# A two-block kernel on one core: weights loaded in exchanged 32-wide blocks and turned in place by VectorE, and the attention's constants made in the second group

## What is computed

```python
xn = _layernorm(x)
s = _L0_attn_ref(xn, W_in, W_out, A_theta, B_real, B_imag, C_real, C_imag, norm_w)
g = _silu(_L0_ffn_ref(xn, W1, W2, W3))   # silu(xn W1^T) * (xn W3^T), Walsh-Hadamard transform over 1024, times W2^T
x = x + s * g
xn = _layernorm(x)
s = _L1_attn_ref(xn, qkv, o_proj, gamma, beta)   # causal softmax attention
g = _silu(_L1_ffn_ref(xn, W1, W2, W3))
x = x + s * g
```

## Time and profile before

| | |
|---|---|
| time, median of 3 runs | 363.39 us (362.97 to 363.65) |
| time of the profiled execution | 363.3 us |
| its span | 361.5 us |
| TensorE busy | 355.8 us, 98% |
| VectorE busy | 250.6 us, 69% |
| ScalarE busy | 169.2 us, 47% |
| GpSimd busy | 100.8 us, 28% |
| granted TensorE clock | 1.0 in every slice (2.4 GHz, the upper level) |
| DMA packets | 42336, of which 5700 under 512 B; 38.63 MB |

### The profile page before, as it was taken

How to read it: one execution, slowest core, us unless ns; L and a number is a source line. 1 busy time by engine, 2 the same in 40 slices (tenths; PEclk the granted TensorE clock), 3 DMA queues, 4 the chain that set the end, 5 groups by cost and what they waited for, 6 DMA issues and landing times.

```text
span 361.5 us, 5052 instructions
## 1 busy us (share of the span) xinstructions
PE 355.8 (98%) x1821; PEld 301.5 (83%) x1821; DVE 250.6 (69%) x481; ACT 169.2 (47%) x335; POOL 100.8 (28%) x126
## 2 busy tenths in 40 slices
PE   7999999999999999999999999999999999999996
PEld 4878888888888888888988878888888888888896
DVE  5669965886489647868568894788646887356645
ACT  2865371355135623554275544644446354454510
POOL 2154410246014723467506030060300603004000
PEclk9999999999999999999999999999999999999999
DMA  7995110525145623440242401424204332054001
GB/s 239 287 320 198 60 59 0 176 58 170 35 133 159 190 74 117 120 145 0 72 134 67 141 0 60 151 54 126 81 30 160 74 117 88 0 190 111 20 3 58
DMA packets 42336, 38.63 MB, mean 107 GB/s; under 512 B 5700, under 2 KB 41800, under 8 KB 42312
## 3 DMA queue, kind: packets, MB, share of 16 engines
q1 hardware_dynamic: 42168, 38.25, 34.8%
q10 hardware_dynamic: 144, 0.07, 0.1%
HBM read 24.09 MB, written 14.22 MB: 106 GB/s over the span
## 4 chain that ended last, share of the span: by engine, by line
PE 94%; DMA 3%; DVE 1%; SPq 1%; issue 0%; ACT 0%
PE GU L362 19%; PE GU L363 19%; PE GU L364 19%; PE O L362 8%; PE O L363 8%; PE O L364 8%; DMA stage<-in_L_ffn_W 3%; PE O L369 1%; PE T L369 1%; PE O L433 1%; PE T L362 1%; PE T L364 1%; PE T L363 1%; PE O L519 1%; PE O L518 1%; PE O L517 1%
## 5 line engine op out<-in xcount | busy, mean ns | idle before, releaser
L730 ACT ACTIVATE hf<-GU 128x512 f32<-128x512 f32 x64 | 38.2, 599 | 80.3 <-DVE hid L854 55.8
L1001 DVE TENSOR_TENSOR hf<-hf,GU 128x512 f32<-128x512 f32 x64 | 43.6, 681 | 32.5 <-PE GU L364 27.1
L362 PE MATMUL GU<-XT,W1T 128*128 128x512 f32 x128 | 50.8, 397 | 0.0
L364 PE MATMUL GU<-XT,W1T 128*128 128x512 f32 x128 | 49.9, 390 | 0.0
L363 PE MATMUL GU<-XT,W1T 128*128 128x512 f32 x128 | 49.9, 390 | 0.0
L362 PE MATMUL GU<-XT,W3T 128*128 128x512 f32 x128 | 49.9, 390 | 0.0
L364 PE MATMUL GU<-XT,W3T 128*128 128x512 f32 x128 | 49.8, 389 | 0.0
L363 PE MATMUL GU<-XT,W3T 128*128 128x512 f32 x128 | 49.8, 389 | 0.0
L854 DVE TENSOR_TENSOR hid<-hf,hid 128x512 fp32r<-128x512 f32 x64 | 48.2, 754 | 1.2 <-ACT hid L661 0.8
L362 PE MATMUL O<-hid,W2hi 128*128 128x512 f32 x112 | 44.0, 393 | 0.0
L363 PE MATMUL O<-hid,W2hi 128*128 128x512 f32 x112 | 43.7, 390 | 0.0
(11 more groups left out here) (204 smaller groups left out, 741.2 us busy)
## 6 DMA issues: line engine op xcount, KB each, us to landing
stage<-in_L_ffn_W SPq DMA_DIRECT2D x24, 256.0 KB, 5.6
swap_rows<-GX SPq DMA_DIRECT2D x7, 512.0 KB, 3.6
sT<-swap_rows SPq DMA_DIRECT2D x28, 128.0 KB, 2.7
swap_gate<-GX SPq DMA_DIRECT2D x7, 512.0 KB, 2.9
sT<-swap_gate SPq DMA_DIRECT2D x28, 128.0 KB, 2.7
swap_p<-PX SPq DMA_DIRECT2D x4, 640.0 KB, 3.2
PL<-swap_p SPq DMA_DIRECT2D x16, 160.0 KB, 3.2
swap_w<-GX SPq DMA_DIRECT2D x4, 512.0 KB, 2.9
```

Source lines behind the costliest of these rows:

```text
L362: pe.matmul(o, lhs(0), rhs(0), start=start, stop=False)
L364: return pe.matmul(o, lhs(1), rhs(0), start=False, stop=stop)
L730: act.activation(hf[:, c % 2, :], GU[:, c % 2, 0, :], ACT.Silu).then_inc(silu_done, 1)
L1001: dve.tensor_tensor(hf[:, c % 2, :], hf[:, c % 2, :], GU[:, c % 2, 1, :], ALU.mult).then_inc(mul_done, 1)
```

## The change

All of W1 and W3 but pair 0, the second block's W2, W_out and qkv are loaded as 32x32 blocks whose positions are already exchanged (four DMAs of 32 partitions each, with runs of 32 numbers), and VectorE turns each block where it lies (`in_place`). GpSimd now makes the low parts of these weights (`pair_lo`, `nat_lo`). ScalarE's queue issues the DMAs of `ssm`, `win`, `normB` and `gbrow`, and ScalarE scales `win`. `small_av` moves into group 1, after up chunk 1. The row loads of x are split in three, the last two with new places in the SP queue. The rows are normalised by `scalar_tensor_tensor` with the reciprocal deviation as a second operand in place of `tensor_scalar`. The way of the second block's weights through DRAM (`move_w`) is gone.

```diff
+            def load_blocks(to, src, done):
+                blocks = src.rearrange("(d b) (c q a) -> q b c d a", b=Q, q=QUADS, a=Q)
+                for q in range(QUADS):
+                    sp.dma_start(to[q * Q:(q + 1) * Q].rearrange("b (c d a) -> b c d a", d=D // Q, a=Q), blocks[q]).then_inc(done, 16)
...
+            load_w(1, 0)
+            load_w(1, 1)
+            load_w2(1)
+            for w in (0, 1):
+                sp.wait_ge(w_tr, w + 1)
+                load_w(2, w)
             sp.wait_ge(w2_tr, 1)
+            load_w2(2)
+            reload_w(3)
...
+            load_blocks(U2[1][:, :, :].rearrange("p c d -> p (c d)"), W2[1], w2_loaded)
             move_rows(1)
...
             def up_chunk(l, n, c, first):
                 if first and c % 2 == 0:
-                    pe.wait_ge(w_lo, c + 2)
+                    pe.wait_ge(wx_lo, c)
...
             def small_m():
-                pe.wait_ge(kstep, KSTEPS)
-                pe.wait_ge(sm_nat, 2)
+                pe.wait_ge(win_scaled, MC)
+                pe.wait_ge(wout_turned, MC // 2)
```

TensorE's program of the head:

```diff
             def block0_head():
...
-                head_pair(0)
+                first_pair()
                 first_x_transposes()
-                head_pair_w2(0)
-                head_pair(1)
+                pair_w2(0)
                 first_up_chunk()
-                head_hadamard(0)
-                head_pair_w2(1)
+                hadamard(0)
+                pair_w2(1)
                 up_chunk(0, 0, 1, True)
-                head_hadamard(1)
-                head_pair(2)
-                head_pair_w2(2)
                 up_chunk(0, 0, 2, True)
+                hadamard(1)
+                pair_w2(2)
                 up_chunk(0, 0, 3, True)
...
                 up_chunk(0, 0, 7, True)
-                small_av()
                 pe.wait_ge(sm_lo, 1)
                 recurrent_mix(0)
...
             def normalise(n, x_at):
-                    last = dve.tensor_scalar(rows2[n % 2][:, t, :], X[:, bass.ds(x_at + t, 1), :].rearrange("p a d -> p (a d)"),
-                                             mv[:, t, 0:1], rstd[:, t:t + 1], ALU.subtract, ALU.mult)
+                    last = dve.scalar_tensor_tensor(rows2[n % 2][:, t, :], X[:, bass.ds(x_at + t, 1), :].rearrange("p a d -> p (a d)"),
+                                                    mv[:, t, 0:1], rstd[:, t:t + 1].broadcast_to([P, D]), ALU.subtract, ALU.mult)
```

and GpSimd's:

```diff
             def block0_head():
...
+                pair_lo(1)
                 pair_butterfly(0, 0, 1)
+                pair_lo(2)
                 pair_butterfly(0, 1, 2)
                 quad_butterfly(0, 0, 4)
+                pair_lo(3)
                 pair_butterfly(0, 2, 3)
                 rstd_of(1)
                 pair_butterfly(0, 3, 4)
```

More of the change, by code:

```diff
@@ L325, in _ @@
                 move_gate(n - 1)
-                for j in ((0,), (1, 2), (3,))[n - 1]:
-                    move_w(PAIRS + j)
+                if n == 2:
+                    reload_w(PAIRS + 3)
                 if n == NB - 1:
@@ L420, in small_natural, with small_gb @@
+            def small_gb():
                 pe.wait_ge(small_loaded, 16 * N_SMALL)
-                pe.wait_ge(w_lo, 2 * PAIRS)
-                for h in (0, 1):
-                    transposes(T[:, h, :], [wout[:, a, (2 * h + m) * P:(2 * h + m + 1) * P] for m in (0, 1) for a in range(KC)]).then_inc(sm_tr, 1)
                 pe.wait_ge(w2nat_ready, PAIRS)
@@ L636, in _ @@
             pe.wait_ge(const_ready, 2)
+            pe.wait_ge(sm_lo, 3)
             block1_group(NB, 0)
@@ L679, in pair_u, with nat_hi, small_hi @@
                 act.activation(U[l][:, 2 * j:2 * j + 2, :].rearrange("p a d -> p (a d)"), O[:, 1, :], ACT.Copy, scale=float(H) ** -0.5).then_inc(u_ready, 1)
-            def nat_hi(i, nat):
-                if not (isinstance(i, int) and i == 0):
+            def nat_hi(i):
+                if i:
                     act.wait_ge(h_done, i)
-                hi(nat[:, 0, :, :].rearrange("p a d -> p (a d)"), O[:, 0, :], w2_tr, i + 1, w2nat_hi)
-            def small_hi(first, n, wait, value, done):
-                for q in range(n):
-                    dst, src = first[q]
-                    hi(dst, src, wait, value + q, done)
+                hi(w2nat[:, 0, :, :].rearrange("p a d -> p (a d)"), O[:, 0, :], w2_tr, i + 1, w2nat_hi)
+            def small_hi(q):
+                R, bank = ((MR, O[:, 0, :]), (AR, T[:, 0, :]), (VR, T[:, 1, :]))[q]
+                hi(R[:, 0, :, :].rearrange("p k d -> p (k d)"), bank, sm_mm, q + 1, sm_hi)
             def w2_hi(l):
@@ L888, in k_vector @@
                 dve.tensor_reduce(kvec[:, :], kprod[:, 0, :, :], AX_X, ALU.add).then_inc(kvec_ready, 1)
-                dve.wait_ge(kvec_ready, 1)
-                for m in range(MC):
-                    dve.tensor_scalar(win[:, m, :], win[:, m, :], kvec[:, m:m + 1], None, ALU.mult).then_inc(kstep, 1)
             def small_lo(q):
```

366 lines of the change are left out of this document (176 added, 190 removed).

## The result

The changed kernel takes 385.57 us at the median of 6 runs (384.33 to 388.09), the kernel before 363.33 in the same comparison: 1.062 times as long, 95% interval 1.058 to 1.066. It is slower, as forecast, but by 22.2 us and not by 9.1; the time lies outside the range of 364 to 378.

The account below looks back on a forecast made before the run. The prediction took TensorE's program to bound the kernel, with almost no waits; it summed 363.3 − 6.66 for transposes + waits of 2.5, 2.6, 7.8 and 2.9 = 372.4 us, range 364 to 378.

Parts of the forecast that it names:

- The transposes' worth: Transposes leaving TensorE's program: 4.90 us saved in the head, 1.76 for the second block's W2, 6.66 in all.
- the first rival: Groups' normalise in its new form does not wait for GpSimd; `woutT`'s wait is 2.2 us, time 366.8; chance 0.22.
- The second wait: Head, Hadamard product of pair 3: TensorE waits 2.6 us for W2's low part, queued behind other VectorE work.
- the first wait: Head, chunk 4: TensorE waits 2.5 us for chunk 2's product, delayed by DMA issues on ScalarE's queue; bounds 0 and 6.9.
- The fourth: Down product of group 1: TensorE waits 2.9 us for `W2lo`, now made behind the last low part; bounds 2 and 3.5.
- The first up chunk: Head: it waits for the split rows of x, starting at 10.1 us, so dropping pair 1's transposes gains nothing.
- Third wait: Head, `small_m`: TensorE waits 7.8 us for W_out, turned after four normalised tiles beside GpSimd; bounds 2.2 and 9.
- The step on the rows of group 1: SP ring: rows queue behind small runs at 14 ns, `XT` ready at 62.8, TensorE there at 68.7; cost 0.
- the four waits: TensorE waits ahead of chunk 4, pair 3's Hadamard product, `small_m` and group 1's down product: 2.5, 2.6, 7.8, 2.9 us.
- small runs become the bound: Rival: at 20 ns a run the rows of group 1 come 7 us after TensorE, time 379.4; chance 0.08.
- the forecast's own signs: Expected in the trace: VectorE behind TensorE's waits, `woutT` longest, ScalarE issues moving silus, tiles 6 to 7 us, `XT` in time.
- the term on groups 1 to 3: Later butterflies beside the normalised tiles could cost up to 3 us in group 2; taken as 0.

Follow-up runs that it names:

- experiment 4: Changed kernel with unread products filling TensorE's five waits over 2.5 us, plus 14 more ahead of `small_m`: 383.46 us, 1.057.
- experiment 6: Kernel before, with only the normalise exchanged from `tensor_scalar` to `scalar_tensor_tensor`: 363.79 us, 1.0014.
- experiment 1: Changed kernel with GpSimd held until VectorE's four normalised tiles are done, in the head and groups 1 to 3: 389.52 us, 1.073.
- experiment 7: Changed kernel with `w2nat`'s low part right behind the additions in groups 1 and 2, and GpSimd held for the normalised tiles: 376.44 us, 1.039.
- experiment 8: Changed kernel with the first block's W2 sum, high and low parts made ahead of chunk 7, as before the change: 387.77 us, 1.068.
- experiment 5: Kernel before, with TensorE made to wait for one to three small DMAs ahead of the fourth up chunk of groups 1 to 6: 403.15 us.
- experiment 10: Changed kernel with GpSimd reordered, group 1's rows earlier, W2 split ahead of chunk 7, pair 3's `w2nat` earlier, four ScalarE-queue issues later: 365.78 us, 1.007.
- experiment 2: Changed kernel with the rows of group 1 issued ahead of the load of the second block's W2: 384.19 us, 1.058.

## Why the prediction was wrong

**Right.** The direction, and the reason: waits in the place of transposes. The transposes' worth: 6.66 by the sum, 4.9 of busy time by experiment 4 and 60 instructions fewer; the trace's overlapping ends lie between the two. The new normalise waits for GpSimd like the old one (experiment 6), which takes the first rival's ground (0.22). *The Trainium skill (SBUF — State Buffer, Who interferes with whom) makes two SBUF inputs enough for contention with a GpSimd instruction that reads SBUF; the 6.31 us agree.* The second wait, `w2nat`: 2.6 forecast, 2.70 measured, in part by luck. The forecast let it shrink to 0.3 without the first wait, and that came out at 0.84 and not 2.5; what filled most of the gap is VectorE's low part of chunk 3, 1.63 us beside a butterfly and 0.68 elsewhere, and 0.35 of waiting for X. The fourth, `W2lo`: 2.9 and 2.96. The first up chunk, 10.1 and 10.12.

**Mis-sized.** *First wait,* 2.5 forecast, 0.84 measured. The five issues on ScalarE's queue took 0.40 to 0.53 each, as assumed, and moved the silu of chunk 1 to 16.78 (17.3 forecast). The next four lasted from 20.48 to 22.40, but beside running activations; the silu of chunk 2 came at 22.50, not at 24.0. *Third wait,* 7.8 forecast, 1.34 measured: the four tiles took 4.75 and not 7.2, `woutT` was turned at 41.2 and not at 45.5; and TensorE came to it at 40.0 and not at 37.7, since its chunk 6 took 5.3 us at half clock instead of 2.7.

**The step on the rows of group 1,** "the cost is 0, hidden by the four waits", failed as well, though narrowly: 62.8 forecast, 69.5 measured, with TensorE ready at 66.2 rather than 68.7, so 3.3. From 56.77 (the issue of `swap_rows`) to 63.15 (the gathers) took 6.4, where the same pair for the gate, with an empty stream, took 2.9; so the small runs ahead ended at about 60.3 rather than 54.4. Spread over the 2432 runs of the forecast that is an estimate of 16.4 ns each (34.0 + 5.9 over 2432), not 14. By the forecast's own numbers that, and not 17, is the point from which they decide (68.7 less 62.8 over 2432 is 2.4 ns). But it is no price of a DMA engine, and here the forecast's picture was wrong: it counted the engines' time alone, and for six of these microseconds they had room (a share of 0.62, where the earlier trace rows have 1.06), while the SP queue issued a quarter every 0.63 us:

```profile
45.00:51.00 6.00, 5.61 (x37) 4.92 (x35) 3.73 (x5) 2.35 (x4) 0.00 (x0) 1.00 0.62 98
```

From 37.70 to 56.73 this queue did nothing but issue the twenty quarters. How much of the lateness is its issuing and how much the engines is not separated. Experiments 1, 4, 7 and 8 show the rows deciding, with waits of 2.62 to 6.69 for them. The rival "small runs become the bound" (0.08) described this mechanism with a price too high: rows 7 us late, where they were 3.3 late and cost 1.7 of half clock behind. Of the forecast's own signs two failed: `woutT` was not the longest wait, and `XT` of group 1 came after TensorE wanted it.

**The step that failed:** the term on groups 1 to 3, "Later butterflies of GpSimd beside the normalised tiles could cost up to 3 us in group 2. I take 0." TensorE waited 3.66 in group 2, 3.10 in group 3 and 0.63 in group 1. Two mechanisms stand behind these. In groups 1 and 3 it is the contention: I had priced it in the head with the very rows 7 and 8 and did not walk the same four tiles through group 3, where three butterflies (1.6, 1.5 and 2.4 us) had newly come to stand beside them; with GpSimd held, the tiles took 1.63 to 1.67 and both waits were gone (experiment 1). In group 2 it is GpSimd's order, which the forecast did not lay out at all: `w2nat` stands behind four butterflies and a pair's splits, and without the contention its wait grew. Experiment 7 gives these microseconds back by GpSimd's order and holds alone.

**The term that was missing:** the clock. The sum prices a wait at its length. In the kernel before the granted clock is 1.00 everywhere, so no row of it showed the price; I treated its absence from the trace as zero and gave it no bounds. It is 8.9 us of the changed kernel by experiment 4. Side by side: the sum had 15.8 of waits and 6.66 off for the transposes; measured are 19.0 of idle time, 4.9 off, and 8.9 of clock, together the 23.0. *The Trainium skill (TensorE: Matmul & The Clock Gate, HAM oscillation — how this bites in real kernels) describes just this: waits that return TensorE to the low clock, to be charged by the time spent there times one half. A forecast with four new waits should have carried that term; the trace agrees in kind (8.9 us).* Had both terms been in the sum, 372.4 + 6.8 for groups 2 and 3 + 1.8 for each of six waits over 2 us (four forecast, two more) would have given 390; the mis-sized third wait would then have been the largest error left.

**What stays open.** Why the best version is still 2 us behind the kernel before: each cure of the head brought the next operand to light (`win`, `beta`, `woutT`, `W2lo`, `MR`), all but `beta`, which a DMA brings, made by VectorE, GpSimd or ScalarE between 30 and 48 us. An order in which none is late was not found; that there is none is not shown. Which waits the low clock follows isn't settled either: 2.96 and 2.97 in experiment 7 and 2.62 in experiment 4 had no low stretch behind them, 2.37 in experiment 5 and 1.57 in experiment 10 had one.

## What to carry to other kernels

When a change swaps work of the bounding engine for waits, price each wait twice: its length, and about 1.8 us more of half clock behind it (all but three of the waits of 1.6 to 8 us here had such a stretch); where it can't be removed, filling it with unread products takes the second price away, provided that nothing late stands right behind. Of two engines that hold each other up, walk every place where they meet, and set the order there so that the one whose result is due next goes first: here that was worth 9 us, without removing an instruction. And find what sets the next group's start before curing the waits ahead of it: the cures of experiments 4 and 8 gained nothing, because TensorE then waited for the rows, and the early rows of experiment 2 gained 1.4 us, because the head was nearly as late.

## What the runs showed of the hardware that was not expected

- A wait of TensorE of 2.4 to 8.2 us was followed by products at a granted clock of 0.50 (128x512 steps of 0.43 us instead of 0.23), costing some 1.8 us a wait on average (1.4 to 2.4 in experiment 5); between 1.6 and 3 us waits with and without such products happened.
- `scalar_tensor_tensor` with one number per row as second input: 415 ns a tile of 128x256 alone, where `tensor_scalar` took 345; beside GpSimd 1.58 us and 1.48 us a tile (four in 6.31 and 5.90).
- A load of 256 x 256 numbers as four DMAs of 512 runs of 128 B occupied the issuing queue for 2.65 us (eight in 5.30 us, 0.66 each), and four with 2048 runs for 5.66 us.
